# One of 52 row gathers per block moved from GpSimd to single-row transfers of SyncE

## The chip, the cores and the metric

One core of one Trainium2 chip. The metric is the device time of one execution in microseconds. Three runs of the kernel before gave 633.69, 634.13 and 634.48 us, median 634.13 us.

## The reference

A recommendation model (DeepFM) on a batch of 2048 samples with 26 categorical and 13 continuous features. Each categorical feature picks one row out of its own table (12500 rows: 64 embedding values and one first-order weight); indices outside the table wrap or are clamped.

```python
emb_cat = cat_t2[fidx, cat_feats]                        # [2048, 26, 64]
emb_cont = cont_t2[None] * cont_feats[:, :, None]        # [2048, 13, 64]
E = concatenate([emb_cat, emb_cont], axis=1)
s = sum(E, axis=1)
fm_second = 0.5 * sum(s * s - sum(E * E, axis=1), axis=1)
h = relu(batchnorm(E.reshape(2048, -1) @ W1 + b1))       # 2496 -> 1024
h = relu(batchnorm(h @ W2 + b2))                         # 1024 -> 512
out_pos = sigmoid(bias + fm_first + fm_second + (h @ W3 + b3))
```

The output is [1 - out_pos, out_pos]. Both batch norms take their mean and variance over the whole batch, so the second layer can't begin before the first layer is done for all 2048 samples.

## The kernel before, in words

The 2048 samples are 16 tiles of 128, taken two at a time: 8 blocks of 256 samples. The 26 features are 13 pairs; pair k of the current block has a slot of `emb` ([128, 2 tiles, 13 x 130] fp32), with samples on partitions. There is one `emb`, so a slot is filled again for the next block once its three readers are done. All row tables are one DRAM tensor `table` of 325000 rows of 65 fp32 (260 bytes).

**GpSimd** (L243 to L262) fills a slot with four indirect DMAs (L255): tile j, feature 2k or 2k+1, 128 rows each, so 52 gathers a block and 416 in all. Before slot k it waits that the readers of the last block are done with it (`summed`, `squared`), that the row numbers are staged (`idx_ready`), and that TensorE is at most AHEAD = 3 slots behind (`transposed`; 5 in block 0). Each gather adds 16 to `gathered[k]`.

**TensorE** (from L697) runs, per block: `continuous` (L776, 16 short products that also begin the accumulation in PSUM), then for k = 2 to 12 `transpose(b, k)` (L724, two) and `multiply(b, k-2)` (16 products of 128x128 by 128x256, L733), then `finish` (L745): the products of the last two slots bank by bank, and between the banks `misc_products` (L766, L767; they wait for the continuous features of the next block) and the first two transposes of block b+1. In the last block the multiplies catch up with the transposes, so that little is left when the last slot lands. The second layer (L808) follows, and a short end.

**ScalarE** copies each transposed pair to `x_sb` (`x_copy`, L286), sums squares of each slot (`square`, L293), copies the sums out to `h1` (L299), and in each block but the last, behind `x_copy(b, 6)`, squares the continuous features of block b+1 (`cont_squares`, L313 to L315), for which it waits for their transfer (`cont_in`). It does all this in program order. In the last block it waits, behind slot 2, for all eight transfers of W2 (L341) and splits W2 into two parts.

**VectorE** adds the slots up (`add_up`, L486), stages the next block's row numbers (`stage_indices`, L475), and takes the statistics of the sums (`stats`, L525), with the first two slots of the next block between them (`NEXT_AT`).

**SyncE** (L211 to L231) issues plain DMAs in order: indices, W1 (L218, L222), then in a loop one small transfer of continuous features per block (L225), which waits until `continuous` of the block before has used the buffer (`cont_used`), then the eight loads of W2 (L227), and the output. `x_done`, `tp_free` (L186 to L194) say which copy of which slot frees a transpose buffer: transpose k waits for the copy of slot k-3.

Of the kernel before, what the change touches and what calls it, by code (L numbers as in the profile page):

```python
# [19 lines left out]
P = 128  # L20
EPS = 1e-5

TILES = BATCH // P
BT = 2
BLOCKS = TILES // BT
BC = BT * P
# [20 lines left out]
EMPTY = 1  # L47
NORM_PARTS = [(0, 1), (1, 2), (2, 4), (4, 6), (6, 8)]
FM_STEPS = 7
ADDED_EARLY = 8  # L50
PAR = 2 * C1 + 4 * C2 + 2
CROWS = CONT + 1


def build(nc, table, cat, cont_t, cont_tab, cont_diag, w1, w2, b1_row, params, out):
# [52 lines left out]
    stats1 = place("stats1", [P, C1, BLOCKS, 6], f32)  # L108
    mv1 = place("mv1", [P, C1, 2], f32)
    bn1 = place("bn1", [P, 5, C1], f32)  # L110


    kt_bytes = H1 * 4
# [12 lines left out]
    ones = place("ones", [P, 1], f32)  # L126
    out_shift = place("out_shift", [P, 1], f32)


    raw = h1[:, :, :].rearrange("p c (s n) -> p (c s) n", n=H1)  # L130
    STD, RSTD, SCALE, MEAN_SCALE, SHIFT = range(5)
# [6 lines left out]
    with ExitStack() as ctx:  # L138
# [17 lines left out]
        idx_ready = sem("idx_ready")  # L156
        gathered = [sem(f"gathered{k}") for k in range(KT)]
        slot_open = sem("slot_open")
        m_done, m_ready = sem("m_done"), sem("m_ready")
        cnorm_ready, cont_sq_ready, cont_used = sem("cnorm_ready"), sem("cont_sq_ready"), sem("cont_used")  # L160
        transposed, x_ready = sem("transposed"), sem("x_ready")
# [48 lines left out]
        @block.sync  # L210
        def _(sp):  # L211
            first = BT * CAT
            sp.dma_start(idx_all[:, 0:first], cat[:, 0:first]).then_inc(idx_first, 16)
            sp.dma_start(idx_all[:, first:TILES * CAT], cat[:, first:]).then_inc(idx_in, 16)
            rows = w1[CAT * DIM:, :]
            for j in range(CONT_KT):
                held = min(P, CONT * DIM - j * P)
                sp.dma_start(raw[0:held, j, :], rows[j * P:j * P + held, :]).then_inc(wc_in[j], 16)  # L218
            sp.wait_ge(cont_ones, 1)
            sp.dma_start(cont_sb[0:CONT, :], cont_t[:, 0:BC]).then_inc(cont_in, 16)  # L220
            for k in range(KT):
                sp.dma_start(w1_sb[:, k, :], w1[k * P:(k + 1) * P, :]).then_inc(w1_in[k], 16)  # L222
            with sp.Fori(1, BLOCKS) as b:
                sp.wait_ge(cont_used, b + EMPTY)
                sp.dma_start(cont_sb[0:CONT, :], cont_t[:, ds(b * BC, BC)]).then_inc(cont_in, 16)  # L225
            for k in range(C1):
                sp.dma_start(w2raw[:, k, :], w2[k * P:(k + 1) * P, :]).then_inc(w2_in, 16)  # L227
            sp.wait_ge(neg_ready, 1)
            sp.wait_ge(prob_ready, 1)
            sp.dma_start(out, prob[:, :, :].rearrange("p t c -> p (t c)")).then_inc(out_done, 16)  # L230
            sp.wait_ge(out_done, 16)  # L231

        @block.gpsimd
        def _(pool):

            nc.gpsimd.iota(idx_off[:, :], pattern=[[VOCAB, CAT]], base=0,
                           channel_multiplier=0).then_inc(off_made, 1)
            nc.gpsimd.memset(ident[:, :], 1.0).then_inc(ident_zero, 1)
            pool.wait_ge(ident_zero, 1)
            nc.gpsimd.affine_select(out=ident[:, :], in_=ident[:, :], compare_op=ALU.is_equal, fill=0.0,  # L240
                                    base=0, pattern=[[-1, P]], channel_multiplier=1).then_inc(ident_made, 1)

            def gather(b, ahead):  # L243

                for k in range(KT):
                    pool.wait_ge(transposed, b * KT + (KT + k + 1 - ahead))
                    pool.wait_ge(summed, b * KT + (k + 1))
                    pool.wait_ge(squared, b * (BT * KT) + BT * (k + 1))
                    pool.wait_ge(idx_ready, b * KT + (k + 1))
                    pool.sem_inc(slot_open, 1)  # L250
                    for j in range(BT):
                        for half in range(2):
                            at = k * PAIR + half * ROW
                            f = 2 * k + half
                            nc.gpsimd.indirect_dma_start(  # L255
                                out=emb[:, j, at:at + ROW], out_offset=None, in_=table,
                                in_offset=bass.IndirectOffsetOnAxis(ap=idx_now[:, j, f:f + 1], axis=0),
                            ).then_inc(gathered[k], 16)

            gather(0, AHEAD_FIRST)  # L260
            with pool.Fori(1, BLOCKS) as b:
                gather(b, AHEAD)  # L262

        @block.scalar
        def _(act):
            act.dma_start(diag[:, :], cont_diag).then_inc(diag_in, 16)
            act.dma_start(ctab[:, :], cont_tab).then_inc(ctab_in, 16)
            act.dma_start(par[:, :], params).then_inc(par_in, 16)
            act.dma_start(m_sb[CONT:CROWS, :], b1_row).then_inc(b1_in, 16)
            for free in acc_free:  # L270
                act.sem_inc(free, EMPTY)
# [171 lines left out]
        def _(dve):  # L443
            for free in (misc_read, fm_step):
                dve.sem_inc(free, EMPTY)
            dve.sem_inc(summed, KT)
            nc.vector.memset(eps[:, :], EPS).then_inc(eps_ready, 1)
            nc.vector.memset(idx_all[:, TILES * CAT:], 0)
            nc.vector.memset(cont_sb[:, :], 1.0).then_inc(cont_ones, 1)
# [36 lines left out]
            def add_up(b, k):  # L486

                rows = emb[:, :, k * PAIR:(k + 1) * PAIR]
                dve.wait_ge(gathered[k], 16 * 2 * BT * (b + 1))
# [47 lines left out]

            for k in range(LEAD):
                start_block(0, k)
            with dve.Fori(0, BLOCKS - 1) as b:  # L540
                for k in range(LEAD, KT):
                    add_up(b, k)
# [154 lines left out]
        def _(pe):  # L697
# [19 lines left out]
            def transpose(b, k):  # L717
                s = k % TP
                if k == TP:
                    pe.wait_ge(misc_read, b + (1 + EMPTY))  # L720
                pe.wait_ge(gathered[k], 16 * 2 * BT * (b + 1))
# [185 lines left out]
```

## Time and profile before

| | before |
|---|---|
| median of 3 runs | 634.13 us |
| the profiled execution's own time | 633.67 us |
| its span, first to last instruction | 631.9 us |
| TensorE products busy | 571.8 us, 90% |
| TensorE weight loads busy | 460.2 us, 73% |
| VectorE busy | 148.9 us, 24% |
| ScalarE busy | 213.6 us, 34% |
| GpSimd busy | 393.8 us, 62% |
| mean granted TensorE clock | 0.955 |

The profiled execution's own time is 1.8 us over its span: the span runs from the first to the last instruction. Busy times of one engine add up to its share of the span, but a busy engine need not be the one that sets the end: products overlap their weight loads and each other, and GpSimd's instruction here only prepares a gather whose rows land later. What binds is read from who waits for whom, stage by stage. Issues of DMAs by SyncE and ScalarE (SPq, ACTq) and register instructions are in the trace but not in the busy times.

### The profile page before, as it was taken

What the parts mean: (1) busy time and instruction counts of PE and PEld (TensorE: products, weight loads), DVE (VectorE), ACT (ScalarE), POOL (GpSimd) and SP (SyncE); (2) the same over time, 40 slices, a digit from 0 to 9 for tenths busy, and PEclk for the clock granted to TensorE, in tenths of its full rate; (3) what the DMA queues carried; (4) which work ended last, traced back from release to release, by engine and by line L of the source; (5) the groups of instructions that cost most, each with busy time, mean ns of one, the idle gap of its engine ahead of it and who ended that gap; (6) DMA issues with size and microseconds to landing.
All of it is one profiled execution on the core that took longest, in us unless ns stands there. A gap on an engine that the chain in (4) does not pass through costs nothing.

```text
span 631.9 us, 8463 instructions
## 1 busy us (share of the span) xinstructions
PE 571.8 (90%) x2531; PEld 460.2 (73%) x2531; DVE 148.9 (24%) x460; ACT 213.6 (34%) x682; POOL 393.8 (62%) x423
## 2 busy tenths in 40 slices
PE   6999899789977997799879987998799999999998
PEld 1588778568866886688658866776678776888887
DVE  1101120013001211130004100311022204754265
ACT  1323132223222322232223222322223315998565
POOL 5777777777777777777777777777777771000000
PEclk9789979998999899998999899979999999999999
DMA  8952334334332343334423432363233321000000
GB/s 265 372 101 27 28 28 27 27 26 28 26 27 27 27 27 27 26 26 27 27 27 26 28 27 26 27 160 27 27 27 28 27 27 9 1 2 0 1 0 2
DMA packets 18251, 26.79 MB, mean 42 GB/s; under 512 B 7827, under 2 KB 8059, under 8 KB 18236
## 3 DMA queue, kind: packets, MB, share of 16 engines
q0 software_dynamic: 13312, 13.87, 27.9%
q1 hardware_dynamic: 4608, 12.66, 5.7%
q8 instruction: 8, 0.13, 0.1%
q10 hardware_dynamic: 316, 0.07, 0.1%
q14 instruction: 7, 0.06, 0.0%
HBM read 26.56 MB, written 0.02 MB: 42 GB/s over the span
## 4 chain that ended last, share of the span: by engine, by line
PE 38%; DMA 26%; issue 16%; POOL 14%; ACT 2%; DVE 2%; POOLq 1%; ACTq 0%; DVEq 0%; SPq 0%
DMA emb<-in_table,idx_now 26%; PE bank L733 15%; PE bank L808 14%; POOL emb L255 14%; PE bank L776 3%; PE bank L707 2%; PE bank L724 2%; ACT junk L293 1%; DVE bank L494 1%; PE bank L844 1%; DMA h<-in_w 1%; PE bank L766 1%; DVE idx_now L477 1%; PE bank L857 1%; PE bank L767 0%
## 5 line engine op out<-in xcount | busy, mean ns | idle before, releaser
L255 POOL DMA_INDIRECT emb<-in_table,idx_now x416 | 393.1, 945 | 129.7 <-issue 118.4
L733 PE MATMUL bank<-x_sb,w_sb 128*128 128x256 f32 x1664 | 391.4, 391 | 2.4 <-ACT x_sb L286 2.4
L733 PEld LDWEIGHTS bank<-x_sb,w_sb 128*128 128x128 f32 x1664 | 320.8, 197 | 46.1 <-ACT x_sb L286 3.6
L293 ACT ACTIVATE junk<-emb 128x128 bf16<-128x128 f32 x208 | 64.2, 309 | 228.4 <-DMA emb<-in_table,idx_now 216.1
L494 DVE TENSOR_TENSOR bank<-emb,bank 128x260 f32<-128x260 f32 x91 | 39.3, 432 | 323.7 <-DMA emb<-in_table,idx_now 323.7
L724 PE MATMUL bank<-ident,emb 128*128 128x128 f32 x208 | 45.1, 301 | 47.7 <-DMA emb<-in_table,idx_now 47.4
L724 PEld LDWEIGHTS bank<-ident,emb 128*128 128x128 f32 x208 | 24.6, 145 | 76.1 <-DMA emb<-in_table,idx_now 66.7
L286 ACT ACTIVATE x_sb<-bank 128x256 f32<-128x256 f32 x104 | 38.6, 371 | 90.4 <-PE bank L724 90.4
L808 PE MATMUL bank<-hhi,w2hi 128*128 128x512 f32 x128 | 50.8, 397 | 0.0
L808 PE MATMUL bank<-hhi,w2lo 128*128 128x512 f32 x128 | 50.4, 394 | 0.0
L808 PE MATMUL bank<-hlo,w2hi 128*128 128x512 f32 x128 | 39.0, 396 | 0.3 <-DVE hlo L605 0.3
L293 ACT ACTIVATION_READ_ACCUMULATOR junk<-emb (+1 forms) x208 | 38.9, 187 | 0.0
L776 PE MATMUL bank<-cont_sb,m_sb 14*128 14x256 f32 x128 | 38.7, 463 | 0.0
L299 ACT ACTIVATE h<-bank 128x512 f32 (+1 forms) x32 | 19.0, 595 | 56.4 <-PE bank L733 56.4
L528 DVE BATCH_NORM_STATS2 stats<-h x56 | 21.1, 418 | 56.7 <-ACT h L299 56.7
L776 PEld LDWEIGHTS bank<-cont_sb,m_sb 14*128 14x128 f32 x128 | 28.0, 224 | 6.7 <-issue 1.5
L605 DVE TENSOR_TENSOR hlo<-hfull,hhi 128x512 fp32r<-128x512 f32 x32 | 22.1, 690 | 30.8 <-ACT hfull L370 30.8
L362 ACT ACTIVATE hhi<-h,bn 128x512 fp32r<-128x512 f32 x32 | 25.9, 809 | 10.1 <-PE bank L808 7.8
L808 PEld LDWEIGHTS bank<-hlo,w2hi 128*128 128x128 f32 x128 | 23.9, 188 | 6.5 <-DVE hlo L605 0.8
L808 PEld LDWEIGHTS bank<-hhi,w2hi 128*128 128x128 f32 x128 | 24.0, 188 | 6.3 <-issue 0.4
L808 PEld LDWEIGHTS bank<-hhi,w2lo 128*128 128x128 f32 x128 | 24.0, 187 | 5.7
L370 ACT ACTIVATE hfull<-h,bn 128x512 f32<-128x512 f32 x32 | 25.7, 803 | 0.0
(80 smaller groups left out, 173.6 us busy)
## 6 DMA issues: line engine op xcount, KB each, us to landing
emb<-in_table,idx_now POOLq DMA_INDIRECT x416, 3.3
w_sb<-in_w SPq DMA_DIRECT2D x13, 512.0 KB, 17.4
h<-in_w SPq DMA_DIRECT2D x6, 512.0 KB, 7.5
w2raw<-in_w SPq DMA_DIRECT2D x8, 256.0 KB, 5.5
h<-in_w SPq DMA_DIRECT2D x1, 256.0 KB, 12.3
idx_all<-in_cat SPq DMA_DIRECT2D x1, 182.0 KB, 2.9
cont_sb<-in_cont_t SPq DMA_DIRECT2D x8, 13.0 KB
diag<-in_cont_diag ACTq DMA_DIRECT2D x1, 45.5 KB, 2.1
```

The costliest lines, as they stand in the source:

```text
L255: nc.gpsimd.indirect_dma_start(out=emb[:, j, at:at + ROW], out_offset=None, in_=table, in_offset=bass.IndirectOffsetOnAxis(ap=idx_now[:, j ...
L286: nc.scalar.activation(x_sb[:, k, :], tp[k % TP], ACT.Copy).then_inc(x_ready, 1)
L293: nc.scalar.activation(junk[:, :], emb[:, j, k * PAIR + 1:k * PAIR + 1 + P], ACT.Square, accum_out=esq[:, ds(b * BT + j, 1), k]).then_inc( ...
L362: nc.scalar.activation(hhi[:, k, :], src, ACT.Relu, bias=bn1[:, SHIFT, k:k + 1], scale=bn1[:, SCALE, k:k + 1]).then_inc(h_high, 1)
L370: nc.scalar.activation(hfull[:, i % 2, :], h1[:, k, n * NB2:(n + 1) * NB2], ACT.Relu, bias=bn1[:, SHIFT, k:k + 1], scale=bn1[:, SCALE, k:k ...
L494: nc.vector.tensor_tensor(tot, rows, tot, ALU.add).then_inc(summed, 1)
L528: nc.vector.bn_stats(stats1[:, c, ds(b, 1), :].rearrange("p b s -> p (b s)"), h1[:, c, ds(b * BC, BC)]).then_inc(stats1_done, 1)
L605: nc.vector.tensor_tensor(hlo[:, k, :], hfull[:, i % 2, :], hhi[:, k, :].bitcast(f32), ALU.subtract).then_inc(h_split, 1)
L724: done = nc.tensor.transpose(tp[s][:, j * P:(j + 1) * P], emb[:, j, k * PAIR + 1:k * PAIR + 1 + P], ident[:, :])
L733: return nc.tensor.matmul(acc[c], w1_sb[:, k, c * P:(c + 1) * P], x_sb[:, k, :], start=False, stop=stop, skip_group_check=True)
L776: done = nc.tensor.matmul(acc[c], m_sb[:, c * P:(c + 1) * P], cont_sb[:, :], start=(c == HELD[m][0]), stop=False, skip_group_check=True)
L808: done = nc.tensor.matmul(bank2(n, m), w[:, k, cols], x[:, k, :], start=(k == 0 and i == 0), stop=(k == C1 - 1 and i == 2))
```

## The change

In blocks 1 to 7 GpSimd leaves out one gather of slot 12 (tile 1, feature 25). Its 128 rows are fetched by SyncE, one DMA of 260 bytes per row, into one of two staging buffers `row_sb[:, t, :]`, and VectorE copies the 128 x 65 values into the slot. The row numbers for all eight blocks come as one line `cat_rows` on one partition, in a part of `h1` that is not used before the last block; VectorE clamps them with four instructions at the start. SyncE reads the row numbers into registers, 8 at a time. The transfer of the continuous features moves into the middle of a fetch (ahead of row 64), and the fetch of block b waits until VectorE has copied the rows of block b-2. W2's loads stay behind the loop. The readers of slot 12 wait for 3 gathers and for VectorE's copy.

```diff
+ROWS_READ = 8
+ROWS_STEPS = 4
+ROWS_K, ROWS_J, ROWS_HALF = KT - 1, BT - 1, 1
...
+    row_sb = place("row_sb", [P, 2, ROW], f32)
...
+    rows_idx = h1[0:1, C1 - BLOCKS // 2:, BATCH - BC:].bitcast(i32)
...
-            with sp.Fori(1, BLOCKS) as b:
+            def cont_load(b):
                 sp.wait_ge(cont_used, b + EMPTY)
                 sp.dma_start(cont_sb[0:CONT, :], cont_t[:, ds(b * BC, BC)]).then_inc(cont_in, 16)
+            def fetch_rows(i, t):
+                for r0 in range(0, P, ROWS_READ):
+                    if r0 == P // 2:
+                        cont_load(2 * i + t)
+                    _, rows = nc.values_load_multi_w_load_instructions(
+                        rows_idx[0:1, ds(i, 1), t * P + r0:t * P + r0 + ROWS_READ].rearrange("p a n -> p (a n)"),
+                        engines=(mybir.EngineType.SP,), min_val=0, max_val=CAT * VOCAB - 1,
+                        skip_runtime_bounds_check_because="the vector engine clamps them")
+                    for j, row in enumerate(rows):
+                        p = r0 + j
+                        sp.dma_start(row_sb[p:p + 1, t, :], table[ds(row, 1), :]).then_inc(rows_landed[t], 16)
+            sp.wait_ge(rows_step, ROWS_STEPS)
+            fetch_rows(0, 1)
+            with sp.Fori(1, BLOCKS // 2) as i:
+                sp.wait_ge(rows_copied, 2 * i)
+                fetch_rows(i, 0)
+                sp.wait_ge(rows_copied, 2 * i + 1)
+                fetch_rows(i, 1)
...
+                            held = (k, j, half) == (ROWS_K, ROWS_J, ROWS_HALF)
+                            if held and rows_elsewhere:
+                                continue
...
             def square(b, k):
-                act.wait_ge(gathered[k], 16 * 2 * BT * (b + 1))
+                act.wait_ge(gathered[k], 16 * (2 * BT - (k == ROWS_K)) * (b + 1))
+                if k == ROWS_K:
+                    act.wait_ge(rows_copied, b + 2)
...
+            dve.wait_ge(rows_in, 16)
+            x, w = rows_idx, x_sb[0:1, KT - BLOCKS // 2:, :]
+            nc.vector.tensor_scalar(w, x, 0, VOCAB, ALU.is_lt, ALU.mult).then_inc(rows_step, 1)
...
+            def copy_rows(i, t):
+                dve.wait_ge(rows_landed[t], 16 * P * (i + t))
+                at = ROWS_K * PAIR + ROWS_HALF * ROW
+                nc.vector.tensor_copy(emb[:, ROWS_J, at:at + ROW], row_sb[:, t, :]).then_inc(rows_copied, 1)
...
+                    if m == ACC_BANKS - 2:
+                        copy_rows(i, t)
+            whole_block(0, 0, 1, True)
+            with dve.Fori(1, BLOCKS // 2) as i:
+                whole_block(2 * i - 1, i, 0)
+                whole_block(2 * i, i, 1)
```

`whole_block` is the body of VectorE's old loop; TensorE's `transpose` and VectorE's `add_up` get the same two waits as `square`. ScalarE issues one more small transfer at the start (the line of row numbers, 4 KB).

## Rows read from the trace of the kernel before

**Rows 1.** The page: busy times, costliest groups (busy, mean ns of one, idle before), DMA queues.
```profile
PE 571.8 (90%) x2531; PEld 460.2 (73%) x2531; DVE 148.9 (24%) x460; ACT 213.6 (34%) x682; POOL 393.8 (62%) x423
...
L255 POOL DMA_INDIRECT emb<-in_table,idx_now x416 | 393.1, 945 | 129.7 <-issue 118.4
...
q0 software_dynamic: 13312, 13.87, 27.9%
```

**Rows 2.** Timeline of GpSimd: start us, us; the first gather of block 3, of block 4, the last.
```profile
199.87 0.94 POOL L255 DMA_INDIRECT emb<-in_table,idx_now  x1 [0.30 <-issue]
...
264.76 0.94 POOL L255 DMA_INDIRECT emb<-in_table,idx_now  x1 [0.30 <-issue]
...
523.41 0.94 POOL L255 DMA_INDIRECT emb<-in_table,idx_now  x1 [0.30 <-issue]
```

**Rows 3.** Timeline of TensorE, block 3: the transposes of slots 9, 11 and 12, `multiply` 7.
```profile
252.24 0.44 PE L724 MATMUL bank<-ident,emb 128*128 128x128 f32 x2 [1.45 <-DMA emb<-in_table,idx_now]
252.51 3.62 PE L733 MATMUL bank<-x_sb,w_sb 128*128 128x256 f32 x16
...
261.95 0.44 PE L724 MATMUL bank<-ident,emb 128*128 128x128 f32 x2 [1.96 <-DMA emb<-in_table,idx_now]
...
267.07 0.44 PE L724 MATMUL bank<-ident,emb 128*128 128x128 f32 x2 [1.22 <-DMA emb<-in_table,idx_now]
```

**Rows 4.** Timeline of SyncE: the loads of W1, of the continuous features, of W2.
```profile
6.54 15.00 SPq L222 DMA_DIRECT2D w_sb<-in_w  x13
30.34 383.97 SPq L225 DMA_DIRECT2D cont_sb<-in_cont_t  x7
414.52 3.69 SPq L227 DMA_DIRECT2D w2raw<-in_w  x8
```

**Rows 5.** Timeline of TensorE, last block: `multiply` 3; transposes of slots 7, 8, 11 and 12.
```profile
489.42 3.62 PE L733 MATMUL bank<-x_sb,w_sb 128*128 128x256 f32 x16
...
501.81 0.44 PE L724 MATMUL bank<-ident,emb 128*128 128x128 f32 x2 [1.05 <-DMA emb<-in_table,idx_now]
...
508.99 0.38 PE L724 MATMUL bank<-ident,emb 128*128 128x128 f32 x2
...
522.23 0.38 PE L724 MATMUL bank<-ident,emb 128*128 128x128 f32 x2
...
526.86 0.44 PE L724 MATMUL bank<-ident,emb 128*128 128x128 f32 x2
```

**Rows 6.** Timeline of VectorE: its first slot, and the idle time before it.
```profile
16.29 0.43 DVE L491 COPY bank<-emb 128x260 f32<-128x260 f32 x1 [10.27 <-DMA emb<-in_table,idx_now]
```

**Rows 7.** Instructions of L225, L269, L227 on the issuing queues: ns min/median/max.
```profile
L225 SPq FUSED_REGOPS  x7: 37/37/43, 30.2 to 413.9; - x7
L225 SPq MOVE cont_sb<-in_cont_t x7: 29/29/29, 30.3 to 413.9; - x7
L225 SPq DMA_DIRECT2D cont_sb<-in_cont_t x7: 311/312/356, 30.3 to 414.0; - x7
...
L269 ACTq DMA_DIRECT2D m_sb<-in_b_row x1: 306/306/306, 2.3 to 2.3; - x1
...
L227 SPq DMA_DIRECT2D w2raw<-in_w x8: 369/432/441, 414.5 to 417.8; - x8
```

**Rows 8.** DMA issues: KB each, median us from issue to landing.
```profile
w2raw<-in_w SPq DMA_DIRECT2D x8, 256.0 KB, 5.5
...
idx_all<-in_cat SPq DMA_DIRECT2D x1, 26.0 KB, 1.9
...
out<-prob SPq DMA_DIRECT2D x1, 16.0 KB, 1.4
```

**Rows 9.** Timeline of ScalarE, block 3: squares of the continuous features; slot 7.
```profile
238.13 0.40 ACT L315 ACTIVATE cont_sq<-cont_sb 13x256 f32<-13x256 f32 x1
...
242.10 0.31 ACT L293 ACTIVATE junk<-emb 128x128 bf16<-128x128 f32 x1 [3.58 <-DMA emb<-in_table,idx_now]
...
242.93 0.36 ACT L286 ACTIVATE x_sb<-bank 128x256 f32<-128x256 f32 x1
```

More of the change, by code:

```diff
@@ L52, with build @@
 CROWS = CONT + 1
-def build(nc, table, cat, cont_t, cont_tab, cont_diag, w1, w2, b1_row, params, out):
+def build(nc, table, cat, cat_rows, cont_t, cont_tab, cont_diag, w1, w2, b1_row, params, out):
     f32, f32r = mybir.dt.float32, mybir.dt.float32r
@@ L158, in build @@
         slot_open = sem("slot_open")
+        rows_in, rows_step, rows_copied, rows_gathered = (
+            sem("rows_in"), sem("rows_step"), sem("rows_copied"), sem("rows_gathered"))
+        rows_landed = [sem(f"rows_landed{t}") for t in range(2)]
         m_done, m_ready = sem("m_done"), sem("m_ready")
@@ L241, in _, with gather @@
                                     base=0, pattern=[[-1, P]], channel_multiplier=1).then_inc(ident_made, 1)
-            def gather(b, ahead):
+            def gather(b, ahead, rows_elsewhere=False):
                 for k in range(KT):
@@ L257, in gather @@
                                 in_offset=bass.IndirectOffsetOnAxis(ap=idx_now[:, j, f:f + 1], axis=0),
-                            ).then_inc(gathered[k], 16)
+                            ).then_inc(rows_gathered if held else gathered[k], 16)
             gather(0, AHEAD_FIRST)
             with pool.Fori(1, BLOCKS) as b:
-                gather(b, AHEAD)
+                gather(b, AHEAD, True)
         @block.scalar
@@ L268, in _ @@
             act.dma_start(par[:, :], params).then_inc(par_in, 16)
+            act.dma_start(rows_idx, cat_rows).then_inc(rows_in, 16)
             act.dma_start(m_sb[CONT:CROWS, :], b1_row).then_inc(b1_in, 16)
@@ L446, in _ @@
             dve.sem_inc(summed, KT)
+            dve.sem_inc(rows_copied, EMPTY)
             nc.vector.memset(eps[:, :], EPS).then_inc(eps_ready, 1)
@@ L485, in _, with add_up @@
             dve.sem_inc(idx_ready, KT - SCRATCH_KT)
-            def add_up(b, k):
-                rows = emb[:, :, k * PAIR:(k + 1) * PAIR]
-                dve.wait_ge(gathered[k], 16 * 2 * BT * (b + 1))
+            dve.wait_ge(rows_in, 16)
+            x, w = rows_idx, x_sb[0:1, KT - BLOCKS // 2:, :]
+            nc.vector.tensor_scalar(w, x, 0, VOCAB, ALU.is_lt, ALU.mult).then_inc(rows_step, 1)
+            dve.wait_ge(rows_step, 1)
+            nc.vector.tensor_tensor(w, w, x, ALU.add).then_inc(rows_step, 1)
+            dve.wait_ge(rows_step, 2)
+            nc.vector.tensor_scalar(w, w, 0, VOCAB - 1, ALU.max, ALU.min).then_inc(rows_step, 1)
+            dve.wait_ge(rows_step, 3)
+            nc.vector.tensor_scalar(x, w, (2 * ROWS_K + ROWS_HALF) * VOCAB, None, ALU.add).then_inc(rows_step, 1)
+            def add_up(b, k, first=False):
+                rows = emb[:, :, k * PAIR:(k + 1) * PAIR]
+                dve.wait_ge(gathered[k], 16 * (2 * BT - (k == ROWS_K)) * (b + 1))
+                if k == ROWS_K and first:
+                    dve.wait_ge(rows_gathered, 16)
+                    dve.sem_inc(rows_copied, 1)
+                if k == ROWS_K:
+                    dve.wait_ge(rows_copied, b + 2)
                 if k == 0:
@@ L539, in _, with whole_block @@
                 start_block(0, k)
-            with dve.Fori(0, BLOCKS - 1) as b:
+            def copy_rows(i, t):
+                dve.wait_ge(rows_landed[t], 16 * P * (i + t))
+                at = ROWS_K * PAIR + ROWS_HALF * ROW
+                nc.vector.tensor_copy(emb[:, ROWS_J, at:at + ROW], row_sb[:, t, :]).then_inc(rows_copied, 1)
+            def whole_block(b, i, t, first=False):
                 for k in range(LEAD, KT):
-                    add_up(b, k)
+                    add_up(b, k, first)
                     stage_indices(k, (b + 1) * BT)
@@ L720, in transpose @@
                     pe.wait_ge(misc_read, b + (1 + EMPTY))
-                pe.wait_ge(gathered[k], 16 * 2 * BT * (b + 1))
+                pe.wait_ge(gathered[k], 16 * (2 * BT - (k == ROWS_K)) * (b + 1))
+                if k == ROWS_K:
+                    pe.wait_ge(rows_copied, b + 2)
                 pe.wait_ge(x_ready, tp_free(b, k))
@@ L884 @@
     cat = np.ascontiguousarray(x["r_cat_feats"].reshape(P, TILES * CAT))
+    tiles = x["r_cat_feats"].reshape(P, TILES, CAT)
+    cat_rows = np.ascontiguousarray(tiles[:, ROWS_J::BT, 2 * ROWS_K + ROWS_HALF].T.reshape(1, BLOCKS // 2, 2 * P))
     cont_t = np.ascontiguousarray(x["r_cont_feats"].reshape(P, TILES, CONT).transpose(2, 1, 0).reshape(CONT, BATCH))
@@ L892 @@
     arrays = {
-        "table": table.reshape(CAT * VOCAB, ROW), "cat": cat, "cont_t": cont_t, "cont_tab": cont_tab,
+        "table": table.reshape(CAT * VOCAB, ROW), "cat": cat, "cat_rows": cat_rows, "cont_t": cont_t, "cont_tab": cont_tab,
         "cont_diag": cont_diag.reshape(P, CONT_KT * CONT), "w1": x["W1"], "w2": x["W2"],
```

## The prediction

> **What bounds the kernel now.** The page's busy times come first [rows 1]: TensorE is busy for 90% of the span, GpSimd for 62%, and taken alone they would name TensorE. The groups show otherwise: GpSimd's gathers take 945 ns each and sit idle before each for "issue", that is, for nothing another engine does. Its timeline [rows 2] shows the pattern: 0.94 us of work and 0.30 us of gap, without a break. A block of 52 gathers is 264.76 - 199.87 = 64.89 us, 1.248 each, and from the first of block 3, at 199.87, to the last, at 523.41, the 259 steps take 1.249 us each. All 416 make 519 us, so GpSimd sets the pace until 524 us. TensorE's timeline confirms it: from slot 7 of a block on it stands idle before nearly each transpose until the rows land, 1.45, 1.96 and 1.22 us in the places shown [rows 3].
>
> SyncE has, after W1 (issued by 6.54 + 15.00 = 21.5), only one small transfer a block [rows 4]: it is nearly free, which is what the change spends.
>
> **What the change removes.** One gather in each of blocks 1 to 7, 1.248 us each. The first six move all later work: 6 x 1.248 = 7.49 us, if TensorE follows. It does: it loses its 1.22 us of idle time before slot 12 [rows 3], and keeps that before the other slots. In the last block TensorE waits for rows at slot 7 (1.05 us), but from there it runs at its own pace: slots follow at (522.23 - 508.99) / 3 = 4.41 us, and the transpose of slot 12 comes 526.86 - 522.23 = 4.63 us after that of slot 11 [rows 5]. Only 0.22 us of it is waiting, so the seventh gather gives 0.2. Sum: -7.7 us. Against the profiled execution's own time, 633.67, that is **626.0 us** if everything added stays hidden. (That execution is 0.5 us under the median of the runs, 634.13.)
>
> **What it adds off the path.** Four index instructions of 1024 elements on one partition: 260 elements on each partition take 0.43 us [rows 6], so 1.7 us each and under 7 us in all, inside the 10.3 us VectorE is idle before 16.29; without that cover they would delay its first `add_up`, which has a block of room. VectorE's copies of 128 x 65: less than those 0.43 us, seven in all, beside engines it does not hold. One more issue on ScalarE's queue, 0.31 us [rows 7], ahead of a bias row needed at 20 us. The rows are 896 transfers of 260 bytes; GpSimd's gathers hold the DMA engines 27.9% of the time [rows 1], so there is room. All taken as nothing; my bounds are 0 to 1 us.
>
> **What SyncE must now do, and in what time.** Per row it must turn a row number into an address and issue one DMA. The only transfer in the trace with an address from a register is L225: 37 ns of register arithmetic, 29 ns of MOVE, 311 ns for the DMA [rows 7]. A DMA onto one partition (L269) took 306 ns, so fewer bytes or partitions hardly help. Between instructions lies at least 0.034 us: W2's eight issues fill 3.69 us at 0.432 each [rows 7, 4]. I take 0.038, a little more, since the gaps beside register instructions are not shown. Per row then 0.377 + 3 x 0.038 = 0.491 us; the lower bound, were the arithmetic and the MOVE gone, is 0.306 + 0.035 = 0.341. For 128 rows: 62.8 us, at least 43.7.
>
> Then 16 reads of eight numbers from SBUF into registers, which the trace does not show. Lower bound: a register instruction with its gap, 0.07 us. Upper: a whole small transfer from issue to landing, 1.4 us [rows 8]. I take 0.6, nearer to the transfer than to the register instruction because it too is a trip to memory and back, but without a write and a semaphore at the far end. That is 9.6 us, bounds 1.1 and 22.4. One fetch: 62.8 + 9.6 = **72.4 us**, with ends at 44.8 and 85.2. A block, with 51 gathers, would be 63.65 us. SyncE doesn't fit.
>
> The Trainium skill (DMA: Bandwidth & Descriptors, Latency and other measured facts) gives a floor of about 600 ns for a `tensor_load`. No run here shows it; by that figure alone the fetch would be an estimated 62.8 + 9.6 = 72.4 us or longer.
>
> **Where lateness reaches the path.** Two things hang on SyncE. The rows themselves have room: VectorE's wait for them holds back only `stats` and `add_up(b, 1)` onward, which GpSimd needs a block later, and the last rows, landed at 21.5 + 7 x 72.4 + 1.9 = 530 us, come before slot 12 of the last block (527 - 9, and the 51 us of delay found below). But the transfer of the continuous features now stands in the middle of each fetch. ScalarE waits for it behind `x_copy(b-1, 6)`, and with it wait `square` and `x_copy` of slot 7, then TensorE's `multiply` 7, then GpSimd, which may be 3 slots ahead only.
>
> From 21.5 us SyncE never rests, so the continuous features of block 7 are issued at 21.5 + 6.5 F, F being one fetch. They land 1.9 us later [rows 8], and the copy of slot 7 of block 6 ends another 1.9 us on: 0.40 for the squares, 243.29 - 242.10 = 1.19 for `square` and `x_copy` [rows 9], and the semaphores, 0.3. Today, `multiply` 7 of block 3 starts at 252.51 [rows 3]; in block 6 of the changed kernel that is 252.5 + 3 x 64.89 - 7.5 = 439.7. Idle time that TensorE can use up behind it: 1.96 + 1.22 in that block, and 1.05 + 0.22 in the last one [rows 3, 5], 4.5 together; with the smaller waits that the rows don't show I take 4.8. So the delay of the end is 21.5 + 6.5 F + 3.8 - 439.7 - 4.8 = 6.5 F - 419.2. It is zero at F = 64.5; at 72.4 it is 51.4 us. In earlier blocks the same sum is smaller, as SyncE loses 8.75 us anew in each.
>
> W2's loads come behind the seventh fetch: 21.5 + 7 F, plus 3.7 to issue, 5.5 to land [rows 4, 8], 1.0 for ScalarE: 538.5. They hold back `x_copy` of slot 3 of the last block, whose product starts at 489.42 today [rows 5]: 42.2 us behind `multiply` 7 of block 6 (252.5 + 194.7 = 447.2), of which some 3.4 is idle time, so 38.9 of work. TensorE would be there at 495.9 + 38.9 = 534.8. That adds 3.7 us. Forecast: 626.0 + 51.4 + 3.7 = **681 us**.
>
> **Rivals.** (1) SyncE keeps up, F at most 64.5: 626.0 us. For it: if the compiler saves the MOVE (0.06 us) or gathers the arithmetic of eight rows, a row costs 0.42 us and the fetch 53 to 55 plus the reads, so reads up to 0.6 us fit; the point of decision is 0.50 us per row, all in. Against it: L225 shows all three instructions in each of 7 turns, and with them the reads may cost 0.1 us only. The Trainium skill (the same page, Issuing engines are not separate DMA queues) calls the sequencer's time to issue a DMA usually small beside the DMA itself. By that rule this case would come out; the trace disagrees for rows so small, where 0.31 us of issue stands against 260 bytes.
>
> (2) It balances: F between 65.5 and 66, the loss of SyncE eats the 7.7 us. 634 us, a narrow window.
>
> (3) The reads cost what a transfer does, 1.4 us: F = 85.2, 626.0 + 134.6 + 10.1 = 771 us. At 1.0 us per read, F = 78.8, it is 626.0 + 93.0 + 6.9 = 726; at 0.3, F = 67.6, 647.
>
> (4) TensorE becomes the bound instead of GpSimd, and the gain is less than 7.7: 627 to 630. TensorE has its waits before slots 7 to 12 of each block, over 6 us, against 1.25 taken; I give this little.
>
> **How the numbers follow.** Forecast case (SyncE too slow, 636 to 726 us): 0.54; slower still: 0.10. Rival 1: 0.31, rival 4: 0.02, together 0.33 for faster; rival 2: 0.03. The likeliest case alone spans 640 to 726; as the faster case holds a third, the range must reach it: 625.3 to 726. A difference below 0.2%, 1.3 us, can't be told from none here.
>
> **What would show it.** In the profile after: the pitch of SPq's row DMAs (0.49 us, and 0.56 with the reads); block length at GpSimd (72 us instead of 64.9, with breaks in its 1.249 us rhythm somewhere behind slot 9); ScalarE idle before the squares of the continuous features until the DMA of `cont_sb` lands; a gap ahead of the W2 split in the last block. If instead GpSimd's rhythm is unbroken and its blocks are 63.65 us, rival 1 holds. The forecast is wrong if a row, reads included, takes under 0.50 us.

## The result and the profile after

The changed kernel takes 656.57 us (655.78 to 657.49, four runs), the one before 634.31 (633.69 to 634.97, four runs): ratio 1.0353, 95% interval 1.034 to 1.0365. It is 22.3 us slower. The forecast was 681, so the direction was right, and the slowdown was put at over twice its size. The profiled execution took 655.78 us.

The page of the changed kernel (busy us, share, instructions; queues; chain; groups with busy, mean ns, idle before):

```profile
PE 576.2 (88%) x2531; PEld 468.8 (72%) x2531; DVE 153.0 (23%) x471; ACT 211.8 (32%) x682; POOL 388.0 (59%) x416
...
q0 software_dynamic: 13088, 13.64, 26.5%
q1 hardware_dynamic: 6400, 12.90, 5.8%
...
SPq 57%; PE 20%; issue 20%; DMA 1%; ACT 1%; DVE 1%; DVEq 0%
...
L289 POOL DMA_INDIRECT emb<-in_table,idx_now x409 | 387.2, 947 | 152.9 <-issue 113.4
L801 PE MATMUL bank<-x_sb,w_sb 128*128 128x256 f32 x1664 | 402.9, 399 | 45.7 <-ACT x_sb L321 45.7
```

GpSimd has done what the change promised: seven gathers fewer and 5.8 us less work than in [rows 1]. Yet it idles 153 us, and the chain that ended last now runs through SyncE's sequencer for 57% of the span. DMA is no busier than before: 26.5% for the gathers, 27.9% in [rows 1], and 5.8% for the queue that now also moves the rows, 5.7% before. What costs is issuing the rows, not moving them.

SyncE's timeline (start, length, line, tile, how many):

```profile
54.58 0.32 SPq L234 DMA_DIRECT2D cont_sb<-in_cont_t  x1
...
122.22 0.32 SPq L234 DMA_DIRECT2D cont_sb<-in_cont_t  x1
...
189.66 0.32 SPq L234 DMA_DIRECT2D cont_sb<-in_cont_t  x1
...
466.26 0.31 SPq L234 DMA_DIRECT2D cont_sb<-in_cont_t  x1
467.58 32.81 SPq L248 DMA_DIRECT2D row_sb<-in_table  x64
500.61 4.55 SPq L258 DMA_DIRECT2D w2raw<-in_w  x8
```

The transfer of the continuous features, in the middle of each fetch, is a clock of SyncE: from 54.58 to 466.26 it ticks six times, (466.26 - 54.58) / 6 = **68.6 us a fetch**. Without the loop's jump it is 67.4 (189.66 - 122.22); where the loop jumps back, twice in these six, it is 70.8 and 70.9, some 3.4 more. Most of that is a pause in which SyncE waits for nothing that the profile shows, in the chain that ended last:

```profile
223.77 2.69 issue
...
362.15 2.73 issue
```

SyncE never rests otherwise, and W2's loads follow at 500.61, 86 us later than in [rows 4].

What a fetch is made of, lines L248 and L242 of the same kernel (duration in ns, min/median/max):

```profile
L248 SPq FUSED_REGOPS  x896: 37/37/51, 21.5 to 500.0; - x180
L248 SPq MOVE row_sb<-in_table x896: 29/29/38, 21.6 to 500.1; - x180
L248 SPq DMA_DIRECT2D row_sb<-in_table x896: 224/225/311, 21.6 to 500.2; - x180
```

```profile
L242 SPq TENSOR_LOAD <-h x112: 684/688/879, 20.7 to 496.4; - x112
L242 SPq FUSED_REGOPS  x96: 51/51/77, 88.4 to 496.3; - x96
```

A row is the three instructions foreseen from [rows 7], but the DMA takes 225 ns, not the 311 that the lone one of L225 showed (the first row's takes 311, and the first behind a read mostly 259 to 263). The pitch of the rows is 0.409 us, of which 0.118 are the gaps. A read takes 0.69 us, 0.81 with its arithmetic and gaps.

Whom it holds up: the changed kernel's waits (us in total, times, longest) and two rows of ScalarE's timeline (idle before in brackets).

```profile
ACT cont_sq L352 <- DMA cont_sb<-in_cont_t: 124.0, 7, 23.9
```

```profile
467.75 0.41 ACT L352 ACTIVATE cont_sq<-cont_sb 13x256 f32<-13x256 f32 x1 [17.81 <-DMA cont_sb<-in_cont_t]
...
511.03 0.63 ACT L379 ACTIVATE w2hi<-w2raw 128x512 fp32r<-128x512 f32 x1 [10.35 <-DMA w2raw<-in_w]
```

ScalarE waits for the continuous features in all seven blocks, 124 us in all, and once 10.35 us for W2. Its waits reach GpSimd, whose rhythm breaks ahead of the first gather of blocks 3 to 7, by 1.62 to 7.90 us, for block 7 by 3.73 us:

```profile
472.27 0.94 POOL L289 DMA_INDIRECT emb<-in_table,idx_now  x1 [0.30 <-issue]
476.95 0.94 POOL L289 DMA_INDIRECT emb<-in_table,idx_now  x1 [3.73 <-ACT junk L330]
```

TensorE stands idle too, and then runs slower for a while. Its `multiply` 7 of block 6, after a wait of 7.07 us, in the changed kernel, then the same products in the kernel before; last, a stretch of the changed kernel (from:to, length, busy times, granted clock, DMA share, GB/s):

```profile
469.31 6.39 PE L801 MATMUL bank<-x_sb,w_sb 128*128 128x256 f32 x16 [7.07 <-ACT x_sb L321]
```

```profile
447.21 3.62 PE L733 MATMUL bank<-x_sb,w_sb 128*128 128x256 f32 x16
```

```profile
465.00:474.00 9.00, 4.69 (x11) 3.79 (x12) 1.01 (x4) 3.99 (x20) 6.38 (x7) 0.50 0.30 28
```

The granted clock was 0.50 there, the lower of its two levels, and one more `multiply`, at 499.33, took 4.97 us, partly at 0.50 (498.6 to 502.1). At the higher level each takes 3.62, so the two lost 2.77 + 1.35 = 4.1 us.

### The profile page after: what moved, and what is told of

Same layout as the page of the kernel before. It is cut to its first block, busy times and chain, and to the rows that moved or that the text cites. A ratio compares the mean times of both kernels' runs of the same rounds, so it can differ in the third digit from the quotient of the medians.

```text
span 654.0 us, 11358 instructions
## 1 busy us (share of the span) xinstructions
PE 576.2 (88%) x2531; PEld 468.8 (72%) x2531; DVE 153.0 (23%) x471; ACT 211.8 (32%) x682; POOL 388.0 (59%) x416
## 3 DMA queue, kind: packets, MB, share of 16 engines
q0 software_dynamic: 13088, 13.64, 26.5%
## 4 chain that ended last, share of the span: by engine, by line
SPq 57%; PE 20%; issue 20%; DMA 1%; ACT 1%; DVE 1%; DVEq 0%
SPq L248 41%; PE bank L876 13%; SPq L242 13%; PE bank L801 5%; SPq L231 2%; DMA w2raw<-in_w 1%; PE bank L912 1%; SPq L227 1%; SPq L258 1%; PE bank L925 0%; SPq L234 0%; ACT x_sb L321 0%; PE bank L792 0%; DVE mv L660 0%; ACT hhi L399 0%
## 5 line engine op out<-in xcount | busy, mean ns | idle before, releaser
L289 POOL DMA_INDIRECT emb<-in_table,idx_now x409 | 387.2, 947 | 152.9 <-issue 113.4
L801 PE MATMUL bank<-x_sb,w_sb 128*128 128x256 f32 x1664 | 402.9, 399 | 45.7 <-ACT x_sb L321 45.7
L801 PEld LDWEIGHTS bank<-x_sb,w_sb 128*128 128x128 f32 x1664 | 328.2, 202 | 94.5 <-ACT x_sb L321 48.5
L321 ACT ACTIVATE x_sb<-bank 128x256 f32<-128x256 f32 x104 | 38.9, 374 | 142.3 <-PE bank L792 141.4
L792 PE MATMUL bank<-ident,emb 128*128 128x128 f32 x208 | 43.3, 292 | 21.6 <-DMA emb<-in_table,idx_now 20.3
L792 PEld LDWEIGHTS bank<-ident,emb 128*128 128x128 f32 x208 | 26.7, 144 | 41.1 <-DMA emb<-in_table,idx_now 30.3
L352 ACT ACTIVATE cont_sq<-cont_sb 13x256 f32<-13x256 f32 x8 | 3.3, 413 | 124.0 <-DMA cont_sb<-in_cont_t 124.0
L581 DVE BATCH_NORM_STATS2 stats<-h (+1 forms) x56 | 21.1, 418 | 91.0 <-ACT h L336 91.0
L844 PE MATMUL bank<-cont_sb,m_sb 14*128 14x256 f32 x128 | 34.9, 428 | 0.0
L844 PEld LDWEIGHTS bank<-cont_sb,m_sb 14*128 14x128 f32 x128 | 25.7, 205 | 5.9 <-issue 1.3
```

The source lines that it names most:

```text
L289: nc.gpsimd.indirect_dma_start(out=emb[:, j, at:at + ROW], out_offset=None, in_=table, in_offset=bass.IndirectOffsetOnAxis(ap=idx_now[:, j ...
L321: nc.scalar.activation(x_sb[:, k, :], tp[k % TP], ACT.Copy).then_inc(x_ready, 1)
L792: done = nc.tensor.transpose(tp[s][:, j * P:(j + 1) * P], emb[:, j, k * PAIR + 1:k * PAIR + 1 + P], ident[:, :])
L801: return nc.tensor.matmul(acc[c], w1_sb[:, k, c * P:(c + 1) * P], x_sb[:, k, :], start=False, stop=stop, skip_group_check=True)
L844: done = nc.tensor.matmul(acc[c], m_sb[:, c * P:(c + 1) * P], cont_sb[:, :], start=(c == HELD[m][0]), stop=False, skip_group_check=True)
```

## The experiments

Theory A: the end comes late because SyncE needs 68.6 us a fetch, through the continuous features first and W2 second. Rival B: the rows themselves, or something that they do to GpSimd or to the memory, hold the kernel. The changed kernel's own trace speaks against the GpSimd part of B: outside the breaks its gathers start 1.249 us apart, as before. Runs fell on different chips. Only h1 and h2 ran where the kernel before takes what it takes above (635.4 us); all others ran on chips where it takes 743 to 752 us, and each is compared with it on its own chip.

**W2 early (e1, e5).** Its loads stand ahead of the first fetch instead of behind the last.

```
+            for k in range(C1):
+                sp.dma_start(w2raw[:, k, :], w2[k * P:(k + 1) * P, :]).then_inc(w2_in, 16)
             sp.wait_ge(rows_step, ROWS_STEPS)
...
-            for k in range(C1):
-                sp.dma_start(w2raw[:, k, :], w2[k * P:(k + 1) * P, :]).then_inc(w2_in, 16)
```

> Edit: W2's eight loads are issued right behind W1's, ahead of the first row fetch; all else as in the changed kernel. My theory (SyncE is late, and its lateness reaches the path at the transfer of the continuous features first and at W2's loads second): the loads put 4.5 us ahead of all seven fetches, so the continuous features of block 7 are issued at 466.3 + 4.5 = 470.8 us and the end moves out by 4.5 us; in exchange ScalarE's 10.4 us wait for W2 in the last block, worth some 4 us of the end, is gone. Together 656 us, no change against the changed kernel (655.8 to 657.5). Rival A (only W2's lateness counts): 645 us or less. Rival B (the traffic of the small transfers slows the gathers): 656 us as well.

> The first kernel again, W2's loads ahead of the row fetches, because on the chip of the first four runs the kernel before took 742.9 us instead of 634.3 and SyncE's fetches of 128 rows took 104 to 124 us instead of 68. On a chip where the kernel before takes 634: my theory 656 us (4.5 us lost ahead of the fetches, some 4 us won at W2's wait); rival A (only W2 counts) 645 or less.

945.45 us beside 742.91 (1.2756, 1.2698 to 1.2813), and 959.59 beside 751.99 (1.2808, 1.2732 to 1.2884). Neither expectation had a figure for a chip where the loss is over 200 us.

**The two kernels again on such a chip (f1, f2).** No edit: the kernel before and the changed one.

> The kernel before, unchanged, on one of the chips where it takes some 745 us. It tells what is slower there: if it is the instruction streams of the queues that stall (as SyncE's did, 0.7 us at a time), GpSimd's gathers keep their 1.249 us pitch inside a run of them and the 110 us lie in pauses; if it is the gathers or the DMA engines, the pitch itself is longer, 1.5 us.

> The changed kernel on the same chip. My theory: the end is set by SyncE, at about the issue of the continuous features of block 7 (21.5 + 6.5 F) plus the rest of block 6 and block 7; with F = 105 us as in the versions run there, 704 us plus about 190 = 890 to 960 us, ScalarE waiting over 250 us for the continuous features. Rival (whatever slows the kernel before there slows this one equally): 656 x 745 / 634 = 771 us.

The kernel before came out at 749.96, ratio 0.9987 (0.994 to 1.0034); the changed one at 969.49, ratio 1.2902 (1.2567 to 1.3236). So the loss there is the change's own. What makes the kernel before slower there are pauses, not slower gathers: in f1 a gather takes 948 ns and the pitch is 1.252 us, and 39 breaks of the rhythm hold 110 us. Line L248 of the changed kernel on that chip shows it:

```profile
L248 SPq FUSED_REGOPS  x896: 1/37/1419, 21.4 to 812.0; - x180
L248 SPq MOVE row_sb<-in_table x896: 2/29/1392, 21.5 to 812.0; - x180
L248 SPq DMA_DIRECT2D row_sb<-in_table x896: 2/225/1399, 21.6 to 812.1; - x180
```

The medians are the same 37, 29 and 225 ns; the greatest are 1.4 us where they were 0.05, 0.04 and 0.31. SyncE's instructions stall there now and then, mostly by some 0.7 us, and a fetch takes (758.90 - 95.49) / 6 = 110.6 us. When they stall can be read from the same trace. GpSimd stands still from 625.7 to 658.1 (its wait is 32.41 us); the issues of the rows in 20 us of this pause, then in 20 us with gathers running:

```profile
L248 SPq DMA_DIRECT2D row_sb<-in_table x40: 224/225/260, 628.3 to 648.0; - x40
...
L248 SPq DMA_DIRECT2D row_sb<-in_table x21: 3/225/707, 670.1 to 689.9; - x21
```

Over the whole trace, reads included, rows in GpSimd's pauses of over 2.5 us follow each other at 0.56 us (495 rows), those beside running gathers at 1.24 us (328 rows). In the changed kernel's trace above it is 0.53 us beside gathers. It is not TensorE: with GpSimd in a pause and TensorE busy a row takes 0.52 us. So nearly all stalls come while GpSimd gathers; what links the two was not found. These chips still serve as an amplifier of SyncE's time, but the length of a fetch is not fixed there: the less the fetches hold GpSimd up, the longer they get (f3 and g2 below).

**Fewer rows (e8, f3).** A fetch of 112 and of 64 rows; the remaining rows of the slot are left at zero. In f3 the features go ahead of row 32.

```
-                for r0 in range(0, P, ROWS_READ):
+                for r0 in range(0, ROWS_GOT, ROWS_READ):
```

> The changed kernel with only the first 112 of the 128 rows fetched per block; the last 16 rows of that gather are left at zero. A fetch is then 2 groups of 8 rows, 8.2 us, shorter: F = 60.4 instead of 68.6 us, below a block's 63.65. My theory (loss = 6.5 F - 419.2 and W2's term, zero below F = 64.5): 626.0 to 627 us; ScalarE's waits for the continuous features almost gone. Rival B (slope of six fetches from a bound at 63.65): the same 626, so this one only tests that SyncE's time is the cause. Rival C (traffic): 12.5% less traffic, 653 us.

> The changed kernel with 64 of the 128 rows per block, the rest of that gather left at zero, the continuous features ahead of row 32. On this chip a fetch is then about 52 us, below a block. My theory (SyncE's time per fetch against the block is the cause): no more than the kernel before on the same chip, 735 to 745 us, and ScalarE's waits for the continuous features gone. Rival B (the traffic or the waits for VectorE's copy are the cause): still over 800 us.

112 rows: 903.89 us (1.2058, 1.1985 to 1.213). 64 rows: 753.83 (1.0059, 0.9991 to 1.0127), no difference from before that can be told. So 128, 112 and 64 rows a fetch give 969, 904 and 754 us. From 128 to 112 (f2 and e8, two such chips) the last continuous features go out 758.90 - 697.68 = 61.2 us earlier, W2's loads 813.49 - 736.27 = 77.2 us, and the profiled execution ends 975.34 - 901.48 = 73.9 us earlier, between the two: the end follows SyncE. With half the rows SyncE is level with GpSimd, though a fetch takes 77.7 us where 52 was expected, some 1.2 us a row, as beside running gathers above. Half the traffic takes away not half the loss but nearly all of it, which is what A says.

**The continuous features ahead of row 8 instead of row 64 (e2, e6), and with W2 early (e3, e7, e9).**

```
-                    if r0 == P // 2:
+                    if r0 == ROWS_READ:
```

> Edit: the transfer of the continuous features stands ahead of row 8 of a fetch instead of row 64; W2's loads stay last. My theory: ScalarE's waits for the continuous features (124 us in the changed kernel) vanish nearly, since the transfer of block 7 is issued at about 437 us instead of 466. But W2 still lands at 511 us, where ScalarE would want it at about 473, so the last block takes over the whole loss: product 3 of the last block at 512 instead of 482 us, less 1.3 of idle time, 626.0 + 29 = 655 us. No gain from this edit alone either. Rival A (only the continuous features count, W2 does not): 627 us. Rival B (the rows themselves are late and hold slot 12): over 640 us, with TensorE and ScalarE waiting at slot 12 for VectorE's copy in every block.

> The second again, continuous features ahead of row 8. My theory: 655 us, because W2, landed at 511 us, takes over the loss in the last block. Rival A (only the continuous features count): 627 us. Rival B (the rows themselves are late): over 640 us with ScalarE and TensorE waiting at slot 12.

> Edit: both of the former, W2 early and the continuous features ahead of row 8. My theory: neither consumer of SyncE is late any more; the last rows land at about 507 us, before slot 12 of the last block (518). 626 to 627.5 us, faster than the kernel before (634.3). Rival B (rows are late, or SyncE's 68 us per fetch against 63.65 us per block must cost its difference six times, 26 us): 650 us. Rival C (traffic slows the gathers): 630 us or more, with GpSimd's pitch above 1.249 us.

> The third again, both edits. My theory: 626 to 627.5 us. Rival B (SyncE's 68 us per fetch against blocks of 63.65 us must cost the difference each time): 650 us. Rival C (the traffic of single rows slows the gathers): 630 us or more with GpSimd's pitch above 1.249 us.

> Both edits together once more (W2's loads ahead of the row fetches, continuous features ahead of row 8), because the two chips so far ran even the kernel before in 743 and 752 us, with stalls of about 0.7 us in SyncE's instruction stream. On a chip where the kernel before takes 634 us: my theory 626 to 627.5 us; rival B (68 us per fetch against 63.65 per block must cost its difference each time) 650 us; rival C (the traffic slows the gathers) 630 or more with GpSimd's pitch above 1.249 us. On a chip where it takes 745, SyncE's fetch again takes over 100 us and the run tells the same as before: about 920.

Alone: 947.3 us (1.2795, 1.2731 to 1.2859) and 960.99 (1.2805, 1.2716 to 1.2893), the same as with W2 early alone. Together: 915.86 (1.2328, 1.2254 to 1.2403), 930.55 (1.2414, 1.2339 to 1.2488) and 928.32 (1.2395, 1.2308 to 1.2482). The second edit bought about 30 us on top of either one alone: the second wait stands right behind the first. The changed kernel itself ran on one of these chips only, e9's; there the two together are 969.49 - 928.32 = 41 us, and what one alone gives isn't measured. In e6 the features went out at 716.94 instead of 758.90 (f2, another such chip), and ScalarE then waited 52.6 us for W2. What is left in e7 is seen in its waits:

```profile
DVE emb L597 <- DMA row_sb<-in_table: 489.2, 7, 74.2
...
ACT cont_sq L352 <- DMA cont_sb<-in_cont_t: 279.7, 6, 51.1
```

With fetches over 100 us no place in the fetch is early enough.

**The continuous features on ScalarE's queue (e4).** SyncE then has nothing but the rows and, ahead of them, W2.

```
+            def cont_load(b):
+                act.wait_ge(cont_used, b + EMPTY)
+                act.dma_start(cont_sb[0:CONT, :], cont_t[:, ds(b * BC, BC)]).then_inc(cont_in, 16)
...
+                    if k == LEAD + 1:
+                        cont_load(b + 1)
```

> Edit: W2 early, and the transfer of the continuous features issued by ScalarE behind slot 3 of the block before; SyncE only fetches rows. My theory: 626.0 us, or up to 1 us less than the version with both edits on SyncE, since SyncE saves 7 x 1.2 us and the features no longer depend on it; ScalarE spends 0.35 us a block, hidden. Rival B: 650 us. Rival C: 630 or more.

947.97 us (1.2802, 1.2743 to 1.286): 32 us slower than e3 on the same chip. The wait moved to the rows, 619.6 us in VectorE's copy L597, and although SyncE has less to issue, its 896 rows take 792 us where e3's take 767. My expectation missed that: taking the first consumer away only exposes the next one of the same late engine. Why the fetches get longer still isn't shown, beyond what f2 shows of rows beside gathers.

**Rows fetched and not used (g1).** All 52 gathers stay; SyncE fetches the rows, and VectorE copies them into a spare tile (with e4's edits).

```
-                nc.vector.tensor_copy(emb[:, ROWS_J, at:at + ROW], row_sb[:, t, :]).then_inc(rows_copied, 1)
+                nc.vector.tensor_copy(spare[:, :], row_sb[:, t, :]).then_inc(rows_copied, 1)
```

> GpSimd makes all 52 gathers of every block as in the kernel before; SyncE still fetches its 128 rows per block, but VectorE copies them into a spare tile and nobody else waits for them. The continuous features are issued by ScalarE, W2 early. What is left of the change is the traffic of 896 single rows and SyncE's time. My theory: within 1% of the kernel before on the same chip (634, or 752 where it takes that), but for VectorE's wait at the copy where SyncE needs over 80 us a fetch: there VectorE falls behind its slots and some 200 us of the loss stay, 940. Rival C (the traffic slows the gathers): slower by 2% and more also where a fetch takes 68 us, with GpSimd's gathers above 0.945 us each.

965.38 us (1.3027, 1.2932 to 1.3123), where 940 was expected for such a chip. The kernel isn't free of the rows, since the copy still stands in VectorE's program:

```profile
DVE spare L593 <- DMA row_sb<-in_table: 676.1, 7, 105.8
...
POOL emb L284 <- DVE idx_now L514: 207.3, 15, 41.3
```

VectorE waits for the rows, and GpSimd for the indices that VectorE prepares behind them. One thing it does show against B: beside 896 row transfers a gather takes 947 ns, as on that kind of chip without them (948).

**Rows in every other block only (g2).** Blocks 1, 3, 5 and 7, four gathers saved, with e4's edits.

> SyncE fetches the gather of slot 12 for blocks 1, 3, 5 and 7 only (nothing left out, GpSimd makes it in the others), the continuous features issued by ScalarE, W2 early. A fetch of 68 us (105 on the slow chips) has two blocks, 128 us (150), so SyncE is never late. My theory: 4 gathers less, 3 x 1.248 + 0.2 = 4.0 us off: 630.2 us where the kernel before takes 634.3, and 0 to 4 us under it where it takes 752. Rival B (a fetch beside the blocks costs by itself): no faster than before, or slower. Rival C (traffic): half the loss it would show in the kernel whose rows nobody uses.

755.67 us, 1.0194 (1.0139 to 1.0248). Four fetches of 128 rows took 594 us, 148 each where 105 was expected, since the rows mostly stand beside gathers, where a row takes 1.24 us as in f2. VectorE still waited for rows three times, 165.9 us. The loss shrinks from 29% to 2% but no gain comes.

**Both edits, and reads of sixteen, on a chip like that of the result (h1, h2).** h1 is e3's kernel. h2 has e4's edits and

```
-ROWS_READ = 8
+ROWS_READ = 16
```

> The transfer of the continuous features stands ahead of row 8 of each fetch instead of row 64, and the loads of W2 ahead of the first fetch. Theory (a fetch costs SyncE 68.6 us, and only these two transfers reach the path): where the kernel before takes 634 us, this takes 626 to 628, since the last rows land at about 500.4 + 3.7 + 1.9 = 506 us, ahead of slot 12 of the last block at 518, and the last continuous features are issued near 441. Rival (the rows themselves are late too, or GpSimd is held by something else): 640 or more. Where the kernel before takes over 740 and a fetch over 100, both say 915 to 930, and the run tells nothing new.

> Eight reads of sixteen row numbers in a fetch instead of sixteen of eight, with the continuous features on the queue of ScalarE and W2 early. Theory (a read costs about 0.69 us for eight registers and little more for sixteen): the fetch gets shorter by some 3 us on a chip where the kernel before takes 634, by 10 or less on the others, and the pitch of the rows inside a read does not change. Rival (a read costs by the number of registers, or each costs a long stall): no change in the fetch, or tens of us.

The kernel before took 635.4 us there (seven runs). h1: **640.06**, ratio 1.0063 (1.0046 to 1.008). It takes back most of the loss, but the 626 to 628 expected did not come. Its SyncE timeline says why:

```profile
20.34 13.05 SPq L251 DMA_DIRECT2D w2raw<-in_w  x8
...
37.66 0.32 SPq L234 DMA_DIRECT2D cont_sb<-in_cont_t  x1
...
451.87 0.31 SPq L234 DMA_DIRECT2D cont_sb<-in_cont_t  x1
```

I had counted W2's eight issues at 3.7 us [rows 4]. Right behind W1's they took 13.05, with a median of 1.73 us each where it was 0.44 behind the last fetch, and the whole chain of fetches begins that much later. By the prediction's own formula (issue of the last features + 3.8 - 439.7 - 4.8) the delay is 451.87 - 440.7 = 11.2 us, and 626.0 + 11.2 = 637.2; its profiled execution took 640.44, on a chip that is 1.3 us slower (635.4 against 634.1). Here too TensorE's granted clock was 0.50 behind the wait for the last features:

```profile
455.10 6.33 PE L801 MATMUL bank<-x_sb,w_sb 128*128 128x256 f32 x16 [7.39 <-ACT x_sb L321]
...
485.12 4.91 PE L801 MATMUL bank<-x_sb,w_sb 128*128 128x256 f32 x16
```

Against 3.62 us each, the two lose 4.0 us, a term that the formula doesn't have. Against the kernel before, the loss falls from 3.5% to 0.6%, some 18 us, and what is left is again SyncE, with the clock behind its waits. Rival B's figure (640 or more) was met, but not by its mechanism: ScalarE still waited 69.3 us for the features, 19.94 before the last of them.

h2: **629.18** (two runs, 628.78 and 629.58), ratio 0.9898 (0.9879 to 0.9918), faster than both kernels, by 1% than the kernel before. With the features off SyncE, a fetch is 64.7 us:

```profile
37.68 452.99 SPq L242 DMA_DIRECT2D row_sb<-in_table  x896
```

```profile
L236 SPq TENSOR_LOAD <-h x56: 1131/1137/1286, 36.3 to 482.9; - x56
```

```profile
L283 POOL DMA_INDIRECT emb<-in_table,idx_now x409 | 388.7, 950 | 127.9 <-issue 114.4
L801 PE MATMUL bank<-x_sb,w_sb 128*128 128x256 f32 x1664 | 389.4, 390 | 2.4 <-ACT x_sb L315 2.4
```

A read of sixteen takes 1.14 us, one of eight 0.69: some 0.24 and 0.056 for each register. My expectation (little more for sixteen) was wrong and its rival near the truth, but halving their number still saves 16 x 0.81 - 8 x 1.26 = 2.9 us a fetch. TensorE's wait for ScalarE falls from 45.7 us to 2.4, and GpSimd is idle 127.9 us instead of 152.9. The gain is 6.2 us where 7.7 was promised; gathers of 950 ns instead of the 945 before, 409 times, would be 2 us of it (the 945 are from another chip). How much of the step from 640 to 629 is due to the reads and how much to the move to ScalarE's queue was not separated, and W2 behind the first fetch was not tried.

## Why the prediction was right, and where it was wrong

**What is removed: right.** h2 brings 6.2 of the 7.7 us once neither ScalarE nor TensorE waits for SyncE. **Rival 4**, a gain of under 7.7 us because TensorE binds, isn't excluded by that; against it, TensorE still waits 46.5 us for rows before its transposes in h2, 47.4 before. DMA room, VectorE's copies (0.2 us each) and the index arithmetic were nothing, as taken.

**SyncE does not fit: right.** The point of decision was 0.50 us a row, all in; measured are 68.6 / 128 = 0.536. Rival 1 fell, narrowly, and with h2's 64.7 us a fetch (0.506) it nearly comes true.

**The price of a row: the step that failed.** "311 ns for the DMA" was taken from lone issues; in a run of issues the same instruction takes 225 ns. The row costs 0.409 us, not 0.491, and 128 of them are 128 x 0.082 = 10.5 us cheaper than forecast. Against it went what I had priced too low: a read at 0.81 instead of 0.6 with everything around it (16 x 0.21 = 3.4 us), and, left out altogether, the features' own issue in the middle of the fetch with its register instructions (0.5) and the loop's jump back (3.4 in two fetches of six, 1.1 on average). 72.4 - 10.5 + 3.4 + 0.5 + 1.1 = 66.9; the rest to the 68.6 measured lies in smaller pauses. The difference of 3.8 us is small, but it enters the end 6.5 times: 6.5 x 3.8 = 24.7 us, which is the miss (681 - 656.6 = 24.4).

**Where lateness reaches the path: right, but for TensorE's clock.** With the measured issue of the last features the same formula gives 466.26 + 3.8 - 439.7 - 4.8 = 25.6 us. Behind W2, TensorE would have been at slot 3 of the last block at 466.26 + 3.8 + 38.9 = 509.0; its product starts where the chain below shows. That is 3.0 us, where 3.7 was forecast. 626.0 + 25.6 + 3.0 = 654.6, and the profiled execution took 655.78. From that product to the end of the span it is 142.05 us, 142.5 before.

The 3.0 us aren't all a wait for W2, though. TensorE stood idle for only 0.34 us before that product: the 4.1 us that it lost at the lower clock, a cost that the prediction left out, had used up the rest. Here W2's lateness covers them, which is luck; its loads alone, made early, would have given some 0.3 us. In h1 nothing covers them. There `multiply` 7 starts 3.2 us behind the issue instead of 3.8, and 637.2 - 0.6 + 4.0 = 640.6, beside 640.44 measured; the chip's 1.3 us would come on top. So the formula holds to some 2 us once the clock is counted.

The chain that ended last, changed kernel (start, length, what):

```profile
504.29 6.71 DMA w2raw<-in_w
511.98 3.72 PE bank L801 x16
```

```profile
511.98 3.72 PE L801 MATMUL bank<-x_sb,w_sb 128*128 128x256 f32 x16 [0.34 <-ACT x_sb L321]
```

The features come first and W2 right behind: the pairs e1/e3 and e5/e7 show the features' part by experiment, e2/e3 and e6/e7 that of W2, and 128, 112 and 64 rows show that the end follows SyncE. All these ran on the chips with the longer fetch; on a chip like that of the result it rests on the traces, h1 and h2.

**The reads against the rules.** The floor of about 600 ns that the Trainium skill gives for a `tensor_load` (DMA: Bandwidth & Descriptors, Latency and other measured facts) agrees with the 0.69 us measured for eight registers. What the same page says of the issue being usually small beside the DMA (Issuing engines are not separate DMA queues) is no guide for a stream of rows of 260 bytes: SyncE's issues, 0.409 us a row, set the time while the DMA engines had room.

**What was to be seen.** ScalarE's idle time before the squares (17.81 us), the break of GpSimd's rhythm (3.73 us) and the gap before the W2 split (10.35 us) are all there. The pitch of the rows with their reads is 0.409 + 0.81 / 8 = 0.51 where 0.56 was written, and a block at GpSimd, from 200.5 to 476.9 in four, is 69.1 us where 72 was.

## What to carry to other kernels

An engine that looks free can be filled by instructions that cost a few tenths of a microsecond each: multiply the full issue sequence (arithmetic, MOVE, DMA, gaps, reads, the loop's jump) by its count before handing it work, and take the DMA's issue from a run of issues, not from a lone one. Whatever else stands in that engine's program, a small input or the weights of the next layer, becomes late with it, and its place in the stream decides the time. Where a backlog adds up over blocks, an error in one round's price counts as often as there are rounds. And where a change makes TensorE wait, price what its products cost at the lower clock behind the wait.

## What the runs showed of the hardware that was not expected

- The same DMA instruction holds the queue 311 ns as a lone issue, mostly 259 to 263 right after a read, and 225 in a run of issues.
- A register read (TENSOR_LOAD) takes 0.69 us for eight registers and 1.14 for sixteen.
- Eight issues of W2 took 13.05 us right behind W1's transfers, and 4.55 behind the last fetch.
- The loop's jump back costs SyncE some 3.4 us where the body holds two fetches, 2.7 of them one pause.
- After TensorE had stood idle for 7.07 us (7.39 in h1) its granted clock was 0.50, and sixteen products took 6.39 us (6.33) instead of 3.62.
- On chips where the kernel before takes 743 to 752 us, SyncE's instructions stall singly, up to 1.4 us, mostly while GpSimd gathers: a row takes 1.24 us beside gathers and 0.56 in GpSimd's pauses (f2), and a fetch of 128 rows a block takes 107 to 112 us where the features stand in it. There the change costs 29% instead of 3.5%. A kernel that leans on one sequencer is the more sensitive to the chip that it meets.
